# Cross attention of a decoder layer on one Trainium2 core: values and queries as three products of high and low parts, with the weights split on GpSimd

## Chip, core and metric

The kernel runs on one core of one Trainium2 chip. The metric is the time of one execution on the device, in microseconds (us). Three runs of the kernel before gave a median of 1062.45 us (1061.57 to 1063.77).

## The reference, cut to what matters

A decoder of two layers works on x (4 batches, 256 tokens, width 128) and a context (4 batches, 512 tokens, width 128). The first layer has a self attention, a cross attention with 16 heads of width 64, and a gated expert block with an attention of its own; the second has a self attention, a cross attention with one head and a mixture. All of it is float32. The change touches the first layer's cross attention alone. With m the normalised context and l the normalised latents (x after the self attention), both 128 wide, it computes

```
kv = concat([m, l], axis=1)                 # (4, 768, 128)
k, v = split(kv @ Wkv)                      # 16 heads of 64 each
q = (l @ Wq)                                # 16 heads of 64
out = softmax(q k^T / sqrt(64)) v           # per batch and head, 256 x 768 scores
y = concat(out) @ Wout
```

## The kernel before

The program is written per engine, with an own instruction list for TensorE, ScalarE, VectorE, GpSimd and the DMA queue of SyncE, and with semaphores between them. Everything lives in SBUF once the packed weights are loaded.

The cross attention is worked off in units. A unit is one pair of heads side (u % 2) of one batch (u // 2): 8 units make one pair of heads, and 8 pairs (XP) make the whole, so there are 64 units. `body(it, prev, cur)` in each engine's list writes out the 8 units of a pair; the first pair stands by itself, the next seven are a hardware loop, and a last partial body drains the pipeline.

Keys and queries of one head are folded into one 128 x 128 matrix per head (`A_all`, made once). A unit's query tile is that matrix times the latents; scores are the query tile times the keys' activations. On TensorE a unit consists of:

- `scores(u, half)` (lines 611 to 618), twice: each is two score tiles of 384 columns, each tile the sum of three products of type float32r (high x high, high x low, low x high), so 12 matmuls of 384 moving columns in a unit;
- `queries(it, u)` (lines 597 to 601), once: one float32 product of 256 moving columns with the stationary `acur`. A float32 matmul is two records in the trace;
- `values(it, b, half)` (lines 603 to 609), once: three float32 products, each with a tile of 128 tokens of `kvT` as stationary and 128 columns of the value weights `wv` moving, six records in the trace;
- `transposed` (lines 620 to 637): 12 transposes of 128 x 128 of the probabilities, one record each;
- in every second unit `weighted` (lines 639 to 648), 12 float32 products in two column halves of the array (24 records), and `factors`, two transposes.

`kvT` (float32) is split once, before the units: ScalarE rounds it to `kv_high` (line 1033), VectorE subtracts to make `kv_low` (line 1414, `key_low`), for each of the four batches. The query tile is split in the same way in each unit: ScalarE copies PSUM to `xq_high` (line 1061, for the first unit line 1026), VectorE makes `xq_low` (line 1408). VectorE also takes the maxima of the scores (line 1419), copies the values out of bank 7 (line 1424) and a third of the transposed probabilities (line 1445); ScalarE does the exponentials (line 1075) and the other two thirds (line 1066).

GpSimd's `cross()` (lines 1755 to 1767) copies the two matrices of the next pair of heads from `A_all` into `acur` (line 1761). Before and after, GpSimd's list holds small jobs of the normalisations (lines 1711 and 1712) and the masked queries of the self attentions (line 1726).

Two waits in front of the first unit matter for the change: the first `queries` and `values` wait for `kvT` alone, and the scores of batch b wait for `kv_split`, which counts the batches of which `kv_low` is there.

Of the kernel before, what the change touches and what calls it, by code (L numbers as in the profile page):

```python
# [14 lines left out]
B = 4  # L15
# [73 lines left out]
def decoder(nc, x_d, ctx_d, mask_d, packs_d, w1_d, w2_d, out_d):  # L89
# [4 lines left out]
    with ctx:  # L94
# [42 lines left out]
        ARENA = 17920  # L137
        arena = sb("arena", [P, ARENA])

# [35 lines left out]
        xprob = area(2, 2 * KEYS)  # L175

        xq_high = sb("xq_high", [P, 2, T], f32r)
        xq_low = sb("xq_low", [P, 2, T], f32r)
        acur = sb("acur", [P, 2, P])
# [149 lines left out]
        sx = family("x", "zT_psum", "zT_act", "zT_dve", "acur_ready", "q_psum", "q_high", "q_ready", "kv_high",  # L329
# [99 lines left out]
        def _(pe):  # L429
# [158 lines left out]
            def cross():  # L588
# [5 lines left out]
                wv, wo = col("v", "wv"), col("v", "wout")  # L594
                W = KEYS // 2

                def queries(it, u):

                    pe.wait_ge(sx["acur_ready"], it * 2 + u % 2 + 1)
                    mm(bank[6][:, T:2 * T], acur[:, u % 2, :], kvT[:, u // 2, S2:KEYS], start=True, stop=True)\  # L600
                        .then_inc(sx["q_psum"], 1)

                def values(it, b, half):

                    for k in range(3):
                        kt = 3 * half + k
                        last = mm(bank[7][:, k * P:(k + 1) * P], kvT[:, b, kt * P:(kt + 1) * P],  # L607
                                  wv[:, bass.ds(it * P, P)], start=True, stop=True)
                    last.then_inc(sx["v_psum"], 1)
# [46 lines left out]

                queries(0, 0)
                for half in range(2):
                    if half:

                        pe.wait_ge(sx["v_ready"], 1)
                    values(0, 0, half)

                def body(it, prev, cur):
                    for u in range(8):
# [3 lines left out]
                        if cur:  # L669
                            pe.wait_ge(sx["q_ready"], n + 1)  # L670
                            if prev or u:

                                pe.wait_ge(sx["exp_done"], n * 2 - 1)
                            if not prev and not odd:

                                pe.wait_ge(sx["kv_split"], b + 1)
                            scores(u, 0)
                            if odd:
                                queries(it + (u + 1) // 8, (u + 1) % 8)

                            pe.wait_ge(sx["v_ready"], n + 2)
                            values(it + (b + 1) // 4, (b + 1) % 4, odd)
# [235 lines left out]
        def _(act):  # L918
# [82 lines left out]
            def cross():  # L1001
# [23 lines left out]
                act.wait_ge(sx["q_psum"], 1)  # L1025
                activation(xq_high[:, 0, :], bank[6][:, T:2 * T], ACT.Copy).then_inc(sx["q_high"], 1)
                act.wait_ge(prep_act, 13)
                act.wait_ge(sx["zT_act"], 1)
                for b in range(B):
                    if b == 2:  # L1030

                        act.wait_ge(sx["zT_dve"], 1)
                    activation(kv_high[:, b, :], kvT[:, b, :], ACT.Copy).then_inc(sx["kv_high"], 1)
# [156 lines left out]
        def _(dve):  # L1190
# [211 lines left out]
            def cross_units():  # L1402
# [58 lines left out]
                v.memset(xrb[:, 0:1], 0.0).then_inc(sx["y_done"], 1)  # L1461
                query_low(1, 0)
                values(1, 0, 0)
                values(2, 0, 1)
                for b in range(B):
# [232 lines left out]
        def _(pool):  # L1698
            done = [0]

            def link(instruction):
                instruction.then_inc(pool_chain, 1)
                done[0] += 1
                pool.wait_ge(pool_chain, done[0])
# [50 lines left out]
            def cross():  # L1755
                def pair(it, prev):
                    for u in range(2):
# [3 lines left out]
                        pool.tensor_copy(acur[:, u, :], A_flat[:, bass.ds(it * 2 * P + u * P, P)])\  # L1761
# [3 lines left out]
                pair(0, False)  # L1765
                with pool.Fori(1, XP + 1) as it:
                    pair(it, True)

            pool.memset(half[:, :], -0.5).then_inc(pool_chain, 1)
            done[0] += 1  # L1770
            pool.wait_ge(pool_chain, 1)
# [99 lines left out]
```

## Time and profile before

| | |
|---|---|
| median of three runs | 1062.45 us |
| the profiled execution, its own time | 1061.55 us |
| its span in the trace | 1059.4 us |
| outside the span | 2.15 us |
| the cross attention's units (from the first scores to the last projection) | about 152 to 567 us of the span |
| a two-unit period in the loop | 12.38 us |

The span is what the profiler sees between the first and the last instruction. Times in the rows are microseconds from the start of the span. For TensorE the trace has two lines of events: PE for the matmuls and PEld for the loads of the stationary operand, which overlap. The duration of a matmul includes the depth of the pipeline, so the durations of neighbours overlap; what a matmul costs in a dense stretch is the distance from its start to the start of the next one. Below, that is called its pitch.

### The profile page before, as it was taken

How to read it: one execution, taken by the hardware profiler on the slowest of the kernel's cores; microseconds unless marked ns; L12 is line 12 of the kernel's file. 1: busy time of each engine (PE TensorE's matmuls, PEld its weight loads, DVE VectorE, ACT ScalarE, POOL GpSimd, SP SyncE). 2: the span in 40 equal slices, each digit the busy share in tenths (PEclk: the TensorE clock that was granted, in tenths of full speed). 3: DMA queues.
4: the chain of work that ended last, by engine and by line, in shares of the span. 5: the costliest groups of instructions: out<-in, count | busy, mean ns of one | idle time of the engine just before them, and what ended most of it. 6: DMA issues, size and time to landing. Idle time of an engine off the chain costs nothing.

```text
span 1059.4 us, 22196 instructions
## 1 busy us (share of the span) xinstructions
PE 979.9 (92%) x7108; PEld 800.9 (76%) x7108; DVE 685.9 (65%) x1715; ACT 573.2 (54%) x1511; POOL 176.3 (17%) x291
## 2 busy tenths in 40 slices
PE   5899979999999999999997999979999888888888
PEld 3677768888888888888884877768999665555665
DVE  5878666556666555666635788853222699999673
ACT  3676556555555555555531677745444376666440
POOL 3434120000000000000002333200000234443100
PEclk9999989999999999999998999999999899999995
DMA  6000000000000000000000000010110000000000
GB/s 254 1 1 0 1 1 1 1 1 1 0 0 0 0 0 0 0 0 0 0 1 0 2 0 0 0 50 21 40 40 30 1 1 0 0 0 0 21 1 20
DMA packets 6402, 12.95 MB, mean 12 GB/s; under 512 B 480, under 2 KB 2528, under 8 KB 5984
## 3 DMA queue, kind: packets, MB, share of 16 engines
q1 hardware_dynamic: 6368, 12.51, 3.5%
q8 instruction: 20, 0.33, 0.1%
q14 instruction: 14, 0.11, 0.0%
HBM read 11.98 MB, written 0.52 MB: 12 GB/s over the span
## 4 chain that ended last, share of the span: by engine, by line
PE 77%; DVE 13%; issue 5%; ACT 2%; DVEq 1%; DMA 1%; POOL 1%; SPq 0%; ACTq 0%
PE psum L504 9%; PE psum L635 8%; PE psum L647 8%; PE psum L769 6%; PE psum L615 5%; PE psum L523 4%; PE psum L617 4%; PE psum L616 4%; PE psum L607 4%; DVE arena L1296 4%; PE psum L600 3%; PE psum L541 3%; DVE arena L1274 2%; PE psum L753 2%; PE psum L754 2%
## 5 line engine op out<-in xcount | busy, mean ns | idle before, releaser
L1419 DVE TENSOR_REDUCE xnegmax<-psum 128x1 f32<-128x768 f32 x128 | 122.4, 956 | 138.5 <-PE psum L617 138.2
L1075 ACT ACTIVATE arena<-psum,xnegmax 128x768 f32<-128x768 f32 x128 | 115.5, 903 | 138.5 <-DVE xnegmax L1419 97.4
L504 PE MATMUL psum<-arena 128*128 (+2 forms) x768 | 187.0, 359 | 1.6 <-ACT arena L970 0.3
L1726 POOL TENSOR_TENSOR arena<-arena,pack_a 128x256 f32 (+1 forms) x192 | 122.6, 647 | 145.6 <-PE psum L508 70.6
L970 ACT ACTIVATE arena<-psum,arena 128x256 f32<-128x256 f32 (+1 forms) x256 | 112.3, 446 | 57.1 <-PE psum L523 26.4
L523 PE MATMUL psum<-pack_a,arena 128*128 128x128 f32 x704 | 110.6, 277 | 29.9 <-ACT arena L977 23.9
L504 PEld LDWEIGHTS psum<-arena 128*128 128x128 f32 x768 | 122.3, 192 | 11.0 <-issue 4.4
L523 PEld LDWEIGHTS psum<-pack_a,arena 128*128 128x128 f32 x704 | 79.3, 141 | 57.9 <-issue 24.2
L635 PE MATMUL psum<-pack_a,arena 128*128 128x128 f32 x768 | 106.8, 275 | 0.2 <-ACT arena L1066 0.2
L615 PE MATMUL psum<-kv_high,xq_high 128*128 128x384 f32 x256 | 101.1, 395 | 1.7 <-DVE kv_low L1414 1.6
L1066 ACT ACTIVATE arena<-psum 128x512 f32<-128x512 f32 x128 | 75.9, 593 | 42.4 <-PE psum L635 42.4
L635 PEld LDWEIGHTS psum<-pack_a,arena 128*128 128x128 f32 x768 | 87.3, 141 | 13.9 <-issue 12.3
L647 PE MATMUL psum<-arena,xv 128*64 128x256 f32 x768 | 89.9, 383 | 0.0
L617 PE MATMUL psum<-kv_high,xq_low 128*128 128x384 f32 x256 | 86.6, 338 | 0.0
L616 PE MATMUL psum<-kv_low,xq_high 128*128 128x384 f32 x256 | 86.5, 338 | 0.0
L1116 ACT ACTIVATE arena<-psum,pack_f 128x512 f32<-128x512 f32 x72 | 49.4, 688 | 60.0 <-PE psum L755 60.0
L769 PEld LDWEIGHTS psum<-arena 128*128 128x128 f32 x576 | 74.7, 191 | 6.1 <-DVE x L1535 0.3
L1303 DVE COPY arena<-psum 128x384 f32<-128x384 f32 (+1 forms) x96 | 59.0, 616 | 26.5 <-PE psum L523 26.5
L647 PEld LDWEIGHTS psum<-arena,xv 128*64 128x64 f32 x768 | 52.3, 137 | 31.0 <-issue 6.0
L769 PE MATMUL psum<-arena 128*128 128x128 f32 x576 | 75.4, 275 | 0.0
L1296 DVE SCALAR_TENSOR_TENSOR arena<-arena,ones_ 128x256 f32<-128x256 f32 x128 | 73.1, 573 | 0.1
L1761 POOL COPY acur<-A_all 128x128 f32 (+1 forms) x18 | 5.7, 321 | 386.4 <-PE psum L600 386.4
(238 smaller groups left out, 1810.1 us busy)
## 6 DMA issues: line engine op xcount, KB each, us to landing
arena<-in_w SPq DMA_DIRECT2D x18, 256.0 KB, 2.8
pack_v<-in_pack_v SPq DMA_DIRECT2D x1, 1088.0 KB, 9.6
pack_l<-in_pack_l SPq DMA_DIRECT2D x1, 1079.5 KB, 12.5
pack_q<-in_pack_q SPq DMA_DIRECT2D x1, 1024.0 KB, 7.4
pack_a<-in_pack_a SPq DMA_DIRECT2D x1, 649.0 KB, 6.2
pack_f<-in_pack_f SPq DMA_DIRECT2D x1, 625.0 KB, 10.6
pack_b<-in_pack_b SPq DMA_DIRECT2D x1, 578.0 KB, 9.3
x<-in_x SPq DMA_DIRECT2D x2, 256.0 KB, 3.2
```

The costliest lines, as they stand in the source:

```text
L504: last = mm(bank[j][:, u * T:u * T + keys], qm[:, j, u * P:(u + 1) * P], kT[:, bass.ds(b * T, keys)], start=True, stop=not a.causal)
L523: last = transpose(bank[4 + j % 2][:, i * P:(i + 1) * P], prob[:, j, u, k * P:(k + 1) * P], ident)
L615: mm(out, xq_high[:, u % 2, tile], kv_high[:, u // 2, keys], start=True, stop=False)
L616: mm(out, xq_high[:, u % 2, tile], kv_low[:, u // 2, keys], start=False, stop=False)
L617: last = mm(out, xq_low[:, u % 2, tile], kv_high[:, u // 2, keys], start=False, stop=True)
L635: last = transpose(bank[4 + (3 * u + c) % 2][:, (2 * i + h) * P:(2 * i + h + 1) * P], xprob[:, u % 2, h * KEYS + kt * P:h * KEYS + (kt + 1 ...
L647: mm(bank[6][XD * a:XD * (a + 1), 0:T], xv[:, b, kt * P + XD * a:kt * P + XD * (a + 1)], xpT[:, b % 2, a, kt * T:(kt + 1) * T], start=(kt ...
L769: last = mm(bank[2 * s + half][:, t * P:(t + 1) * P], hid[:, FT * half + f, t * P:(t + 1) * P], w2b[:, s, f * D:(f + 1) * D], start=(f == ...
L1075: activation(xprob[:, u % 2, half * KEYS:(half + 1) * KEYS].rearrange("p (c w) -> p c w", c=2), src, ACT.Exp, bias=xnegmax[:, u % 2, half: ...
L1296: v.scalar_tensor_tensor(prob[:, j, u, :], eraw[:, j, u, :], low[:, j, u:u + 1], ones[:, :], ALU.max, ALU.min, accum_out=sums[:, it, u * H ...
L1419: v.tensor_reduce(xnegmax[:, u % 2, half:half + 1], banks_pair(half), AX.XY, ALU.max, negate=True)\
L1726: pool.tensor_tensor(qm[:, j, :], qT[:, bass.ds(b * T, T)], headmask[:, bass.ds(g * HG + j, 1)].broadcast_to([P, T]), ALU.mult)\
```

## The change

`queries` becomes three float32r products (high x high, high x low, low x high) of 256 columns, and `values` becomes nine of 128 columns. They read `kv_high` and `kv_low` in place of `kvT`. The stationary of `queries` is now the split matrix `acur_high`/`acur_low`; the moving operand of `values` is the split weight `wcur`, of which there is one copy. Both splits are made on GpSimd: for each of the three 128 x 128 matrices of a pair, an exact copy (into `weff`, which is free by then), a rounding copy and a subtraction.

New waits: the first `queries` waits for `kv_split` 1 (before: for nothing but `kvT`), the values of the next batch in the first pair for `kv_split` b + 2, the values of the next pair (at u = 6) for `wcur_ready`; GpSimd waits for the last values of a pair (`v_psum`) before it overwrites `wcur`. On ScalarE the first query tile's copy moves behind `kv_high` of batch 0, and on VectorE `key_low(0)` moves ahead of the first query tile and the first two value copies.

```diff
@@ tiles
+        CROSS = 17408
+        with nc.sbuf_tensor("before_acur_low", [P, CROSS], f32), nc.sbuf_tensor("acur_low", [P, 2, P], f32r) as acur_low, \
+                nc.sbuf_tensor("wcur", [P, 2, P], f32r) as wcur:
+            pass
         arena = sb("arena", [P, ARENA])
...
-        acur = sb("acur", [P, 2, P])
+        acur_high = sb("acur_high", [P, 2, P], f32r)
@@ pe, cross()
                 def queries(it, u):
 
                     pe.wait_ge(sx["acur_ready"], it * 2 + u % 2 + 1)
-                    mm(bank[6][:, T:2 * T], acur[:, u % 2, :], kvT[:, u // 2, S2:KEYS], start=True, stop=True)\
+                    out, keys = bank[6][:, T:2 * T], slice(S2, KEYS)
+                    mm(out, acur_high[:, u % 2, :], kv_high[:, u // 2, keys], start=True, stop=False)
+                    mm(out, acur_high[:, u % 2, :], kv_low[:, u // 2, keys], start=False, stop=False)
+                    mm(out, acur_low[:, u % 2, :], kv_high[:, u // 2, keys], start=False, stop=True)\
                         .then_inc(sx["q_psum"], 1)
 
                 def values(it, b, half):
 
                     for k in range(3):
                         kt = 3 * half + k
-                        last = mm(bank[7][:, k * P:(k + 1) * P], kvT[:, b, kt * P:(kt + 1) * P],
-                                  wv[:, bass.ds(it * P, P)], start=True, stop=True)
+                        out, keys = bank[7][:, k * P:(k + 1) * P], slice(kt * P, (kt + 1) * P)
+                        mm(out, kv_high[:, b, keys], wcur[:, 0, :], start=True, stop=False)
+                        mm(out, kv_high[:, b, keys], wcur[:, 1, :], start=False, stop=False)
+                        last = mm(out, kv_low[:, b, keys], wcur[:, 0, :], start=False, stop=True)
                     last.then_inc(sx["v_psum"], 1)
...
+                pe.wait_ge(sx["kv_split"], 1)
                 queries(0, 0)
+                pe.wait_ge(sx["wcur_ready"], 1)
...
-                            if not prev and not odd:
-
-                                pe.wait_ge(sx["kv_split"], b + 1)
                             scores(u, 0)
+                            if not prev and not odd and b + 1 < B:
+
+                                pe.wait_ge(sx["kv_split"], b + 2)
                             if odd:
                                 queries(it + (u + 1) // 8, (u + 1) % 8)
 
                             pe.wait_ge(sx["v_ready"], n + 2)
+                            if u == 6:
+
+                                pe.wait_ge(sx["wcur_ready"], it + 2)
                             values(it + (b + 1) // 4, (b + 1) % 4, odd)
@@ act, cross()
-                act.wait_ge(sx["q_psum"], 1)
-                activation(xq_high[:, 0, :], bank[6][:, T:2 * T], ACT.Copy).then_inc(sx["q_high"], 1)
                 act.wait_ge(prep_act, 13)
                 act.wait_ge(sx["zT_act"], 1)
                 for b in range(B):
+                    if b == 1:
+                        act.wait_ge(sx["q_psum"], 1)
+                        activation(xq_high[:, 0, :], bank[6][:, T:2 * T], ACT.Copy).then_inc(sx["q_high"], 1)
@@ dve, cross_units()
                 v.memset(xrb[:, 0:1], 0.0).then_inc(sx["y_done"], 1)
+                key_low(0)
                 query_low(1, 0)
                 values(1, 0, 0)
                 values(2, 0, 1)
-                for b in range(B):
+                for b in range(1, B):
                     key_low(b)
@@ pool, cross()
+                wv, exact = col("v", "wv"), weff[:, :].rearrange("p (i c) -> p i c", i=3)
+
+                def weights(it, prev):
+
+                    if prev:
+
+                        pool.wait_ge(sx["v_psum"], it * 8)
+                    chain.did(pool.tensor_copy(exact[:, 2, :], wv[:, bass.ds(it * P, P)]))
+                    link(pool.tensor_copy(wcur[:, 0, :], wv[:, bass.ds(it * P, P)]))
+                    pool.tensor_tensor(wcur[:, 1, :], exact[:, 2, :], wcur[:, 0, :].bitcast(f32), ALU.subtract)\
+                        .then_inc(sx["wcur_ready"], 1)
+
                 def pair(it, prev):
                     for u in range(2):
                         if prev:
 
                             pool.wait_ge(sx["q_psum"], it * 8 - 1 + u)
-                        pool.tensor_copy(acur[:, u, :], A_flat[:, bass.ds(it * 2 * P + u * P, P)])\
+                        now = A_flat[:, bass.ds(it * 2 * P + u * P, P)]
+                        chain.did(pool.tensor_copy(exact[:, u, :], now))
+                        link(pool.tensor_copy(acur_high[:, u, :], now))
+                        pool.tensor_tensor(acur_low[:, u, :], exact[:, u, :], acur_high[:, u, :].bitcast(f32), ALU.subtract)\
                             .then_inc(sx["acur_ready"], 1)
 
                 pool.wait_ge(prep_act, 5)
                 pair(0, False)
+                pool.wait_ge(loaded["v"], 16)
+                weights(0, False)
                 with pool.Fori(1, XP + 1) as it:
+                    chain.enter(it, 1, 6)
+                    weights(it, True)
                     pair(it, True)
+                    chain.leave(XP)
```

## Rows read from the trace of the kernel before

**Rows 1.** The page, busy time by engine: us (share of the span) x instructions.
```profile
PE 979.9 (92%) x7108; PEld 800.9 (76%) x7108; DVE 685.9 (65%) x1715; ACT 573.2 (54%) x1511; POOL 176.3 (17%) x291
```

**Rows 2.** Windows, 160 to 540 us: length, PE, PEld, DVE, ACT, POOL, PEclk, DMA.
```profile
160.00:540.00 380.00, 379.81 (x2760) 328.57 (x2759) 229.82 (x402) 208.28 (x463) 4.74 (x16) 1.00 0.00 0
```

**Rows 3.** Waits in 160 to 540 us: who waited for whom, us, times, longest.
```profile
DVE xnegmax L1419 <- PE psum L617: 137.4, 93, 3.6
...
PEld psum L635 <- issue: 11.5, 30, 0.4
...
PEld psum L647 <- ACT arena L1066: 1.7, 7, 0.2
```

**Rows 4.** Timeline of PE in the loop: start, duration, line, operands, records.
```profile
455.74 2.81 PE L647 MATMUL psum<-arena,xv 128*64 128x256 f32 x24
...
465.01 0.59 PE L600 MATMUL psum<-kvT,acur 128*128 128x256 f32 x2
465.44 0.83 PE L607 MATMUL psum<-pack_v,kvT 128*128 x6
466.11 1.04 PE L635 MATMUL psum<-pack_a,arena 128*128 128x128 f32 x8
...
467.16 0.34 PE L616 MATMUL psum<-kv_low,xq_high 128*128 128x384 f32 x1
...
467.86 0.34 PE L617 MATMUL psum<-kv_high,xq_low 128*128 128x384 f32 x1
468.12 1.08 PE L647 MATMUL psum<-arena,xv 128*64 128x256 f32 x8
```

**Rows 5.** Timeline, the expert gate's matmuls of 10 moving columns and their successor.
```profile
711.68 1.86 PEld L733 LDWEIGHTS psum<-pack_f,zT 128*128 128x128 f32 x16 [1.25 <-ACT zT L932]
...
713.46 0.19 PEld L753 LDWEIGHTS psum<-z_high,w_high 128*128 128x128 f32 x1
```

**Rows 6.** Groups of weight loads by line and shape: busy us, mean ns of one.
```profile
L647 PEld LDWEIGHTS psum<-arena,xv 128*64 128x64 f32 x768 | 52.3, 137 | 31.0 <-issue 6.0 <-ACT arena L1066 1.7
L616 PEld LDWEIGHTS psum<-kv_low,xq_high 128*128 128x128 f32 x256 | 48.6, 190 | 0.8
L615 PEld LDWEIGHTS psum<-kv_high,xq_high 128*128 128x128 f32 x256 | 48.5, 189 | 5.7 <-issue 1.8 <-DVE xq_low L1408 0.4
...
L541 PEld LDWEIGHTS psum<-arena 128*32 128x32 f32 x768 | 20.3, 109 | 21.2 <-issue 6.6 <-DVE arena L1303 5.8 <-ACT arena L977 0.2
...
L508 PEld LDWEIGHTS psum<-causalb,identb 128*128 128x128 bf16 x256 | 25.4, 99 | 3.3
```

**Rows 7.** Timeline of PE in the experts: float32r products of 512 moving columns.
```profile
727.41 0.39 PE L754 MATMUL psum<-z_low,w_high 128*128 128x512 f32 x1
...
727.65 0.39 PE L755 MATMUL psum<-z_high,w_low 128*128 128x512 f32 x1
...
727.88 1.05 PE L769 MATMUL psum<-arena 128*128 128x128 f32 x8
```

**Rows 8.** Timeline of all engines around the first query and value products.
```profile
145.21 0.99 POOL L1761 COPY acur<-A_all 128x128 f32<-128x128 f32 x2
...
147.76 0.67 PE L600 MATMUL psum<-kvT,acur 128*128 128x256 f32 x2 [0.95 <-DVE kvT L1399]
...
148.75 3.03 ACT L1033 ACTIVATE kv_high<-kvT 128x768 fp32r<-128x768 f32 x4
...
150.80 0.56 DVE L1424 COPY xv<-psum 128x384 f32<-128x384 f32 x1 [1.03 <-PE psum L607]
151.27 3.55 DVE L1414 TENSOR_TENSOR kv_low<-kvT,kv_high 128x768 fp32r<-128x768 f32 x4
...
154.75 0.95 DVE L1419 TENSOR_REDUCE xnegmax<-psum 128x1 f32<-128x768 f32 x1
```

**Rows 9.** GpSimd's copies of 128 x 128: duration ns min/median/max.
```profile
L1761 POOL COPY acur<-A_all x18: 292/296/759, 145.2 to 537.0; 128x128 f32 x16, 128x128 f32<-128x128 f32 x2
```

**Rows 10.** GpSimd's products of 128 x 256: duration ns min/median/max.
```profile
L1726 POOL TENSOR_TENSOR arena<-arena,pack_a x192: 607/614/1076, 16.0 to 970.9; 128x256 f32 x168, 128x256 f32<-128x256 f32 x24
```

More of the change, by code:

```diff
@@ L175, in decoder @@
         xprob = area(2, 2 * KEYS)
+        assert area.at <= CROSS
         xq_high = sb("xq_high", [P, 2, T], f32r)
         xq_low = sb("xq_low", [P, 2, T], f32r)
-        acur = sb("acur", [P, 2, P])
+        acur_high = sb("acur_high", [P, 2, P], f32r)
         xnegmax = sb("xnegmax", [P, 2, 2])
@@ L327, in family @@
             return {n: sem(f"{tag}_{n}") for n in names}
-        sx = family("x", "zT_psum", "zT_act", "zT_dve", "acur_ready", "q_psum", "q_high", "q_ready", "kv_high",
+        sx = family("x", "zT_psum", "zT_act", "zT_dve", "acur_ready", "wcur_ready", "q_psum", "q_high", "q_ready", "kv_high",
                     "kv_split", "v_psum", "v_ready",
@@ L593, in cross @@
                 pe.wait_ge(loaded["v"], 16)
-                wv, wo = col("v", "wv"), col("v", "wout")
+                wo = col("v", "wout")
                 W = KEYS // 2
@@ L1698, in _ @@
         def _(pool):
-            done = [0]
+            chain = Chain(pool_chain)
             def link(instruction):
-                instruction.then_inc(pool_chain, 1)
-                done[0] += 1
-                pool.wait_ge(pool_chain, done[0])
+                chain.did(instruction)
+                chain.wait(pool)
             def rstd_jobs(keys):
@@ L1765, in cross @@
                 pair(0, False)
+                pool.wait_ge(loaded["v"], 16)
+                weights(0, False)
                 with pool.Fori(1, XP + 1) as it:
+                    chain.enter(it, 1, 6)
+                    weights(it, True)
                     pair(it, True)
-            pool.memset(half[:, :], -0.5).then_inc(pool_chain, 1)
-            done[0] += 1
-            pool.wait_ge(pool_chain, 1)
+                    chain.leave(XP)
+            link(pool.memset(half[:, :], -0.5))
             rstd_jobs(FIRST_JOBS)
```

## Prediction

> **What bounds the kernel now.** I read the page's busy shares first: TensorE 92%, the other engines 65% and less [rows 1]. A share over the whole span does not say what bounds one stage, so next the stretch of the cross attention's loop: in 380 us PE is busy 379.8, VectorE 230, ScalarE 208, GpSimd 5, and the granted clock is 1.00, the upper level of 2.4 GHz [rows 2]. The waits of the same stretch say it more clearly: VectorE waits 137 us for TensorE's scores, while TensorE's loads of weights wait for another engine only 1.7 us in total; its other idle time, 11.5 us in front of the transposes, is its own issue [rows 3]. So TensorE bounds the loop, nothing is queued in front of it, and what the change adds or takes in a unit shows in the end time. What counts is therefore the pitch of its instructions, start to start, from the timeline [rows 4].
>
> **The pitches of now.** A values call is six records: 466.11 - 465.44 = 0.67 us, 0.112 each. A queries call takes 465.44 - 465.01 = 0.43 us. A float32r product of 384 columns, with its own load, has a pitch of (467.86 - 467.16)/4 = 0.175 us [rows 4], one of 512 columns 0.235 (727.88 - 727.41 over two) [rows 7]: both are 0.457 ns a column, so at these widths the columns set the pitch.
>
> **What the change does to queries.** Three products of 256 columns: by 0.457 ns a column an estimate of 0.117 us each, 0.35 in all, against 0.43: -0.08 us a unit.
>
> **What it does to values.** Nine products of 128 columns in place of six records, and this is the disputed term. The columns alone would give 9 x 0.058 = 0.53 us. But each product loads its own 128 x 128 stationary, and the trace shows what such a load costs where the moving side is almost nothing: the expert gate's 16 records with 10 moving columns take 713.46 - 711.68 = 1.78 us, 0.111 each [rows 5]. Those are float32 loads. Is a float32r load cheaper? Loads of 128, 64 and 32 columns last 190, 137 and 109 ns [rows 6]: 0.84 ns a column on some 82 ns of fixed latency, so 128 columns occupy the path for 0.108 us, which is the pitch again; and the 190 ns is that of float32r (the scores' lines 615 and 616). The one fast load, 99 ns, is bf16 [rows 6]. Neither does a shared stationary help: the scores' first two products have the same stationary, and the trace holds 256 loads for each of the two lines [rows 6]. So I take 9 x 0.111 = 1.00 us against 0.67: +0.33 us a unit. The ends are 0.058 a product (the column rate, 0.53 a call) and 0.222 (a float32r product as slow as the two float32 records of the same shape [rows 4], 2.0 a call); 0.111 is nearest to both a load and a record of this shape.
>
> Two rules speak otherwise. The Trainium skill, "TensorE: Matmul & The Clock Gate", section "Weight-path perf modes", says that the fast weight load is used for 128 weights when the type is not FP32; if float32r counted as such, the loads would vanish behind the columns and the sum would be that of rival A. The float32r loads' 190 ns beside the 99 ns of bf16 speak against it. The same page, "Back-to-back issue gap", gives about 81 ns for a pair of load and matmul of 128 columns in a real kernel; by it a values call would take 0.73 us and the loop would end within 2 us of today. That is rival B.
>
> **The loop's sum.** (+0.33 - 0.08) x 64 units = +16.0 us. The number of changes between float32 and float32r neighbours stays the same, so I take nothing for them. VectorE and ScalarE get no more work in a unit, and have idle time behind TensorE [rows 3]; the values' copy comes 0.33 us later after TensorE's start, before scores that are as much later.
>
> **GpSimd** gets nine instructions a pair in place of two. Copies of this size take 0.296 us [rows 9]; a product of twice the size 0.614 [rows 10], so a subtraction about 0.31, at most 0.61. The value weights have one buffer: their split can only start when the values of unit 5 are done and must end before those of unit 6. It takes 2 x 0.30 + 0.31 = 0.9 us, 1.2 with the upper end. Between the two calls lie at least 468.12 - 466.11 = 2.0 us and then 24 records of `weighted`, 2.75 us: 4.7 us [rows 4]. The query matrices' split is queued behind it on GpSimd, is due only at unit 7, and costs another 0.9 each. Cover: TensorE's transposes, scores and `weighted`; if a step were late, TensorE would stand still once a pair for the difference. I take nothing.
>
> **The start.** Today `queries` start at 147.76, when `kvT` is there [rows 8]. Now they wait for `kv_high` of batch 0 (3.03/4 = 0.76 us on ScalarE) and `kv_low` (3.55/4 = 0.89 on VectorE): +1.65 us. Two values calls follow one behind the other, through one bank: 2 x 0.33 more. Of the `key_low` calls ahead of the first maximum (154.75 [rows 8]) one is already done: -0.89. Together +1.4 us. GpSimd's first nine instructions start at 145.21 [rows 8] and take some 3 to 4 us, done at about the time at which the first values want them. Ends: 0 (the first units are full of gaps that may take it up) and +4 (two values calls at half the clock, another 1 us each, and GpSimd late by half a us).
>
> **Sum:** +16.0 + 1.4 = +17.4 us on the profiled execution's own time of 1061.55 (span 1059.4 and 2.15 around it), which lies 0.9 below the median. Against the median, 1062.45 + 17.4 = 1079.9 us.
>
> **Rivals.**
> A, faster: the float32r product of 128 columns goes at its column rate, 0.058 us, the load being hidden. Its place is the values call on TensorE; -0.14 - 0.08 = -0.22 a unit, -14.3 + 1.4: 1049.5 us. It decides below a pitch of (0.67 + 0.08)/9 = 0.083 us. For: 384 and 512 columns do run at column rate. Against: rows 5 and 6.
> B, no change: load and product overlap partly, at about the pitch of 0.083 at which the gain of the queries pays for the values: +0 to 2 us, about 1063. Only the cited page speaks for it; the trace has no pair with a full load of this type under 0.11.
> C, much slower: a float32r product of few columns falls back to two slow passes, 0.222 us. +1.33 - 0.08 = +1.25 a unit, +80: 1144 us. Against: nothing at 384 columns hints at it. For: no row has fewer.
> D, GpSimd late: the rounding copies are far slower than plain ones. At 3 us an instruction the split takes 9 us against 4.7 to 6, TensorE stands 3 to 4 us for each of eight pairs: about +28 on top, 1108 us. Against: rows 9 and 10.
>
> **How the numbers follow.** The load-bound case 0.80, A 0.06, B 0.03, C 0.07, D 0.04. The load-bound case's own range: below, the start costs nothing, two or three units are hidden in its gaps and the load counts 0.108 us: some +12 to +14, 1075; above, load and product disturb each other by the 9% that the 384-column pitch (0.175) has over 384 columns at 2.4 GHz (0.160): 0.121 a product, +0.42 - 0.07 = +0.35 a unit, 22.4 + 4 = +26, 1089. I give 1071 to 1090, which holds nearly all of this case and a mild form of D, 0.81 in all. Such a kernel's measurement tells about 0.2%, 2 us, from no change: faster 0.06, same 0.03, slower 0.91.
>
> **What the profile of the changed kernel would show.** Right: nine records of `values` in about 1.0 us and three of `queries` in 0.35; a two-unit period of 12.38 + 0.5 = 12.9 us; PE still without waits in the loop and its clock at 1.00; loads of `values` of 190 ns each; VectorE's wait for the scores longer by some 15 us. The first scores about 1 us later. Wrong: a values call of 0.55 us and a period near 12.0 (A), of 0.75 and 12.4 (B), of 2 us and 15 (C), or an idle TensorE in front of unit 6's values, ended by GpSimd (D). A fall of the granted clock in the loop would make every term too small.

## The result, and the profile after

The changed kernel takes 1076.3 us (median of four runs, 1074.7 to 1077.7) against 1062.8 for the kernel before in the same job: a ratio of 1.0127, 95% interval 1.0109 to 1.0146, so 11.6 to 15.5 us slower. The forecast was 1079.9 us, in a range of 1071 to 1090; 91% stood on slower. The profiled execution has a span of 1072.9 us, 13.5 more than before.

The page, busy time by engine, answers to [rows 1]:

```profile
PE 992.2 (92%) x7371; PEld 821.5 (77%) x7371; DVE 690.7 (64%) x1715; ACT 572.2 (53%) x1511; POOL 197.7 (18%) x354
```

TensorE is busy 12 us longer and has 263 more records; GpSimd is busy 21 us longer, VectorE 5, ScalarE as it was. The same stretch of the loop as [rows 2], with the columns of there, and its waits, which answer to [rows 3]:

```profile
160.00:540.00 380.00, 378.98 (x2931) 337.75 (x2930) 229.47 (x393) 203.15 (x452) 20.32 (x63) 1.00 0.00 0
```

```profile
DVE xnegmax L1435 <- PE psum L627: 134.1, 90, 3.6
...
PEld psum L645 <- issue: 11.2, 29, 0.4
```

TensorE is full as before, at the same granted clock of 1.00. VectorE's wait for the scores, which I had expected to grow by some 15 us, did not: 134.1 us against 137.4. The timeline of PE in the loop, which answers to [rows 4] (L606 to L608 are the three query products, L616 to L618 the nine value products, L645 the transposes, L657 `weighted`):

```profile
451.29 0.28 PE L606 MATMUL psum<-kv_high,acur_high 128*128 128x256 f32 x1
...
451.64 0.23 PE L616 MATMUL psum<-wcur,kv_high 128*128 128x128 f32 x1
451.70 0.27 PE L617 MATMUL psum<-wcur,kv_high 128*128 128x128 f32 x1
451.81 0.28 PE L618 MATMUL psum<-wcur,kv_low 128*128 128x128 f32 x1
...
452.60 1.06 PE L645 MATMUL psum<-pack_a,arena 128*128 128x128 f32 x8
...
454.64 2.81 PE L657 MATMUL psum<-arena,xv 128*64 128x256 f32 x24
...
467.28 2.81 PE L657 MATMUL psum<-arena,xv 128*64 128x256 f32 x24
```

A queries call takes 451.64 - 451.29 = 0.35 us, a values call 452.60 - 451.64 = 0.96, with a pitch of 0.11 between its products; only the first takes 0.06. Its load began at 451.52, under the last query product. The two-unit period is 467.28 - 454.64 = 12.64 us, against 12.38. The groups of weight loads in 160 to 540 us answer to [rows 6]:

```profile
L626 PEld LDWEIGHTS psum<-kv_low,xq_high 128*128 128x128 f32 x244 | 46.2, 189 | 0.0
...
L616 PEld LDWEIGHTS psum<-wcur,kv_high 128*128 128x128 f32 x180 | 34.3, 191 | 0.0
```

The value products' loads last 191 ns, the scores' 189: the same load.

Where the 13.5 us lie, by rows of the chain of waits (first and last mark of each stage: the first self attention's projection, the first block of `weighted`, the cross attention's projection):

```profile
123.27 3.57 PE psum L575 x32
...
171.07 2.74 PE psum L647 x24
...
548.06 7.15 PE psum L716 x64
```

```profile
125.61 3.57 PE psum L580 x32
...
176.38 2.74 PE psum L657 x24
...
561.44 7.15 PE psum L731 x64
```

The first fence is before, the second after. Up to the first mark +2.34 us, in a stage that the change does not touch. From there to the first `weighted` 47.80 and 50.77: +2.97. From there to the projection 376.99 and 385.06: +8.07. Behind it 511.34 and 511.46: +0.12. The first difference is scatter: over the traces of this study that mark lies between 123.1 and 125.6 us, whatever the kernel. The whole time scatters too (the kernel before ran from 1058.2 to 1065.1 us in 23 runs of one job), and the granted clock in stretches outside the loop differs between traces. So the experiments below are read by stage first, and by the ratio second.

### The profile page after: what moved, and what is told of

Read it like the earlier page. It is cut to its first block, busy times and chain, and to the rows that moved or that the text cites. A ratio compares the mean times of both kernels' runs of the same rounds, so it can differ in the third digit from the quotient of the medians.

```text
span 1072.9 us, 22822 instructions
## 1 busy us (share of the span) xinstructions
PE 992.2 (92%) x7371; PEld 821.5 (77%) x7371; DVE 690.7 (64%) x1715; ACT 572.2 (53%) x1511; POOL 197.7 (18%) x354
## 4 chain that ended last, share of the span: by engine, by line
PE 78%; DVE 12%; issue 4%; ACT 2%; DVEq 1%; DMA 1%; POOL 1%; SPq 0%; ACTq 0%
PE psum L509 10%; PE psum L645 8%; PE psum L657 8%; PE psum L784 6%; PE psum L528 5%; PE psum L625 4%; PE psum L626 4%; PE psum L627 4%; DVE arena L1312 4%; PE psum L546 3%; PE psum L618 2%; PE psum L617 2%; PE psum L616 2%; PE psum L768 2%; PE psum L769 2%
## 5 line engine op out<-in xcount | busy, mean ns | idle before, releaser
L528 PEld LDWEIGHTS psum<-pack_a,arena 128*128 128x128 f32 x704 | 79.4, 142 | 58.1 <-issue 24.5
L645 PE MATMUL psum<-pack_a,arena 128*128 128x128 f32 x768 | 108.2, 277 | 0.2 <-ACT arena L1082 0.2
L625 PE MATMUL psum<-kv_high,xq_high 128*128 128x384 f32 x256 | 95.5, 373 | 1.0 <-DVE xq_low L1424 1.0
L645 PEld LDWEIGHTS psum<-pack_a,arena 128*128 128x128 f32 x768 | 84.2, 140 | 13.8 <-issue 12.3
L657 PE MATMUL psum<-arena,xv 128*64 128x256 f32 x768 | 90.0, 383 | 0.0
L657 PEld LDWEIGHTS psum<-arena,xv 128*64 128x64 f32 x768 | 52.3, 137 | 31.1 <-issue 7.9
L1779 POOL COPY weff<-pack_v 128x128 f32 (+1 forms) x9 | 2.6, 292 | 320.8 <-PE psum L618 320.8
```

The source lines that it names most:

```text
L528: last = transpose(bank[4 + j % 2][:, i * P:(i + 1) * P], prob[:, j, u, k * P:(k + 1) * P], ident)
L625: mm(out, xq_high[:, u % 2, tile], kv_high[:, u // 2, keys], start=True, stop=False)
L645: last = transpose(bank[4 + (3 * u + c) % 2][:, (2 * i + h) * P:(2 * i + h + 1) * P], xprob[:, u % 2, h * KEYS + kt * P:h * KEYS + (kt + 1 ...
L657: mm(bank[6][XD * a:XD * (a + 1), 0:T], xv[:, b, kt * P + XD * a:kt * P + XD * (a + 1)], xpT[:, b % 2, a, kt * T:(kt + 1) * T], start=(kt ...
```

## The experiments

All numbers of the loop are means over the 23 to 25 periods between 200 and 500 us of each trace, taken from the start times in the timeline. "Even block" is the stretch of the even unit from the eight transposes through queries, second scores and four transposes to the next scores.

| kernel | time, us | ratio to before (95%) | period | values call | even block | start |
|---|---|---|---|---|---|---|
| before | 1062.8 | | 12.39 | 0.667 | 2.97 | 47.8 |
| after | 1076.3 | 1.0127 (1.0109-1.0146) | 12.65 | 0.955 | 2.68 | 50.8 |
| cols64 | 1076.6 | 1.0134 (1.0110-1.0157) | 12.65 | 0.922 | 2.72 | 51.0 |
| merged | 1063.0 | 0.9995 (0.9979-1.0011) | 12.32 | 0.641 | 2.98 | 50.1 |
| q_only | 1062.2 | 0.9997 (0.9983-1.0011) | 12.32 | 0.665 | 2.95 | 48.6 |
| v_only | 1078.0 | 1.0144 (1.0120-1.0167) | 12.79 | | 2.75 | 53.4 |
| start_only | 1064.6 | 1.0026 (1.0011-1.0040) | 12.40 | 0.667 | 2.97 | 48.9 |
| pool_only | 1064.8 | 1.0022 (1.0010-1.0033) | 12.40 | 0.668 | 2.96 | 48.3 |
| filler | 1067.6 | 1.0041 (1.0027-1.0055) | 12.52 | 0.778 | 2.86 | 48.1 |
| cut_before | 1059.9 | 0.9972 (0.9961-0.9984) | 12.29 | 0.667 | 2.87 | 48.3 |
| cut2_before | 1057.1 | 0.9948 (0.9933-0.9963) | 12.16 | 0.667 | 2.72 | 47.7 |
| cut2_after | 1075.2 | 1.0124 (1.0106-1.0143) | 12.65 | 0.955 | 2.68 | 50.9 |
| best | 1061.3 | 0.9978 (0.9964-0.9993) | 12.33 | 0.666 | 2.96 | 47.8 |
| best2 | 1062.8 | 0.9999 (0.9989-1.0010) | 12.41 | 0.667 | 3.03 | 47.5 |

The first two rows are of one job; in the jobs of the others the kernel before had medians of 1062.7 to 1063.2, and each ratio is to its own job. "Start" is the time from the first self attention's projection to the first `weighted`, by the chain of waits of each trace. In `v_only` the boundary between queries and values in the odd unit isn't comparable, so its values call is left out.

### Load or columns

`cols64`:

```diff
-                        mm(out, kv_high[:, b, keys], wcur[:, 0, :], start=True, stop=False)
+                        mm(out, kv_high[:, b, keys], wcur[:, 0, 0:XD], start=True, stop=False)
...
```

(and so for the other two products).

> The changed kernel with 64 instead of 128 moving columns in each of the nine value products (the other half of each pair's values is left out); everything else, the loads of 128 x 128 stationary tiles too, is the same. Theory (a product of 128 columns costs its load, 0.106 us a product in the changed kernel's loop): the values call stays at 0.95 us, the two-unit period at 12.65 us, the time at 1076 us within 2. Rival (narrow float32r products are slow by the column, 0.83 ns each at this width): the call halves to 0.5 us, the period falls by 0.9 us, the time to about 1048 us.

Measured: the same period and time as the changed kernel, 12.65 and 1076.6 us. The timeline of PE in the loop of `cols64`:

```profile
451.44 0.19 PE L616 MATMUL psum<-wcur,kv_high 128*128 128x64 f32 x1
451.47 0.28 PE L617 MATMUL psum<-wcur,kv_high 128*128 128x64 f32 x1
451.58 0.28 PE L618 MATMUL psum<-wcur,kv_low 128*128 128x64 f32 x1
...
452.36 1.09 PE L645 MATMUL psum<-pack_a,arena 128*128 128x128 f32 x8
```

The pitch of products of 64 columns is 0.11 us, that of 128 columns. (The call counts as 0.92 us in the table, 0.03 less, and the transposes behind it take 0.03 more.) The rival falls: half the columns buy nothing, the product costs its load. The Trainium skill, "TensorE: Matmul & The Clock Gate", section "LDWEIGHTS (loading the stationary operand)", gives the number of stationary columns over 1.2 GHz, 107 ns for 128; the trace agrees within 5%, with 0.955 us over nine products of the changed kernel, 0.106 each, or 0.112 for the eight behind the short first one. The 81 ns for a pair of load and product of 128 columns that the Trainium skill gives on the same page, section "Back-to-back issue gap", is not what these rows show for float32r.

`merged` joins the two products that share their stationary tile:

```diff
-                        out, keys = bank[7][:, k * P:(k + 1) * P], slice(kt * P, (kt + 1) * P)
-                        mm(out, kv_high[:, b, keys], wcur[:, 0, :], start=True, stop=False)
-                        mm(out, kv_high[:, b, keys], wcur[:, 1, :], start=False, stop=False)
-                        last = mm(out, kv_low[:, b, keys], wcur[:, 0, :], start=False, stop=True)
+                        out, keys = bank[7][:, k * P:(k + 2) * P], slice(kt * P, (kt + 1) * P)
+                        mm(out, kv_high[:, b, keys], wcur[:, :, :].rearrange("p i c -> p (i c)"), start=True, stop=False)
+                        last = mm(out[:, 0:P], kv_low[:, b, keys], wcur[:, 0, :], start=False, stop=True)
```

> The changed kernel with the first two value products, which share their stationary tile, as one of 256 moving columns (high and low weights side by side; the low half lands beside its place and is not added, so the output lacks it). Same 9 x 128 columns streamed, six loads in place of nine. Theory (each load costs 0.106 to 0.111 us where it is not covered by columns): a call takes 3 x (0.117 + 0.06 to 0.11) = 0.55 to 0.68 us, the period falls from 12.65 to about 12.0 to 12.1, the time to 1057 to 1060 us. Rival (the columns set the time): 1076 us.

Measured: 0.641 us a call, six loads at 0.107, with as many columns as before. The period falls only to 12.32 where 12.65 - 2 x 0.314 = 12.02 was due. The missing 0.30 us is in the even block, which grew back from 2.68 to 2.98 us though nothing of it was edited. So the loop holds a wait that a long values call hides.

### Each part alone

`q_only`: the value products, `wcur_ready` and the weights' split as before, the rest as changed. `v_only`: the reverse.

```diff
# q_only, against the changed kernel
-                        mm(out, kv_high[:, b, keys], wcur[:, 0, :], start=True, stop=False)
...
+                        last = mm(bank[7][:, k * P:(k + 1) * P], kvT[:, b, kt * P:(kt + 1) * P],
+                                  wv[:, bass.ds(it * P, P)], start=True, stop=True)
# v_only, against the changed kernel
-                    mm(out, acur_high[:, u % 2, :], kv_high[:, u // 2, keys], start=True, stop=False)
...
+                    mm(bank[6][:, T:2 * T], acur[:, u % 2, :], kvT[:, u // 2, S2:KEYS], start=True, stop=True)\
```

> The changed kernel with the values as before (float32 from kvT and wv, six records a call); queries as three products, GpSimd splits the query matrices alone, start as changed. If only the products' own pitch counts (-0.08 us a unit, start +1.4): 1059 us. If, as the two traces together suggest, a float32 product between float32r or transposed neighbours in the even units costs more than its own time (the even unit's queries and what stands on both sides of them lost 0.20 us, the odd unit's 0.08), the period falls from 12.39 to 12.11 us and the time to 1055 us.

> The changed kernel with the queries as before (float32, acur from GpSimd, kvT); values as nine products. If the terms add up as in my sum (values +0.29 a unit, no gain of the queries): 1076 + 5 = 1081 us, period 12.8 us. If the change of type costs about 0.1 us each time that a float32r product follows a float32 one, as the even unit of before shows, the odd unit gains another such place (queries float32, then values float32r): period 12.98 us, 1084 us.

Both of my numbers for `q_only` fail, the second one clearly: 12.32 us a period in place of 12.11. The odd unit's queries gained 0.08 us as computed; the even block gained 0.02 in all, though its queries and the following scores are shorter by 0.08 together. For `v_only` the period of 12.79 is the additive one (12.8), and the whole time is 1078, below both numbers; the change of type as a cost of 0.1 us falls with it. Against the kernel before, though, the period grew by 0.40 where two longer value calls alone make 0.58, and again the even block is short (2.75). The 0.20 us that I had put down to the type had another cause.

### The hidden waits

The timeline of the kernel before in one even unit, all engines:

```profile
460.91 1.04 PE L635 MATMUL psum<-pack_a,arena 128*128 128x128 f32 x8
461.32 0.41 DVE L1428 TENSOR_TENSOR arena<-psum,xrb 128x256 f32 x1
...
461.78 0.30 PEld L600 LDWEIGHTS psum<-kvT,acur 128*128 128x128 f32 x2
...
462.41 0.59 ACT L1066 ACTIVATE arena<-psum 128x512 f32<-128x512 f32 x1
...
462.89 0.38 ACT L1061 ACTIVATE xq_high<-psum 128x256 fp32r<-128x256 f32 x1
...
463.30 0.42 DVE L1408 TENSOR_TENSOR xq_low<-psum,xq_high 128x256 fp32r<-128x256 f32 x1
463.37 0.60 PE L635 MATMUL psum<-pack_a,arena 128*128 128x128 f32 x4
...
463.85 0.19 PEld L615 LDWEIGHTS psum<-kv_high,xq_high 128*128 128x128 f32 x1
463.86 0.44 PE L615 MATMUL psum<-kv_high,xq_high 128*128 128x384 f32 x1
```

Two of TensorE's starts sit right behind another engine. The queries' load (461.78) follows the end of VectorE's scaling of the outputs (461.32 + 0.41 = 461.73), for whose `y_done` they wait. The next unit's scores (463.85) follow the end of `xq_low` (463.30 + 0.42 = 463.72) by 0.13, and `xq_low` stands at the end of a chain: scores, maximum, exponential, ScalarE's copy of transposed probabilities (462.41), its copy of the query tile (462.89). In the changed kernel:

```profile
460.22 0.41 DVE L1444 TENSOR_TENSOR arena<-psum,xrb 128x256 f32 x1
...
460.89 0.19 PEld L606 LDWEIGHTS psum<-kv_high,acur_high 128*128 128x128 f32 x1
...
462.22 0.42 DVE L1424 TENSOR_TENSOR xq_low<-psum,xq_high 128x256 fp32r<-128x256 f32 x1
...
462.41 0.60 PE L645 MATMUL psum<-pack_a,arena 128*128 128x128 f32 x4
...
462.77 0.19 PEld L625 LDWEIGHTS psum<-kv_high,xq_high 128*128 128x128 f32 x1
```

the scaling ends at 460.63 and the queries load at 460.89, when TensorE has come to them, and the four transposes before the next scores take 0.36 us in place of 0.49. Here too the scores' load comes 0.13 after the end of `xq_low` (462.64), but the transposes' loads have only just ended: the chain has no room left. So a start right behind another engine's end does not yet show lost time; the runs below have to.

Hardly any of this is named in the list of waits [rows 3]. A matmul's record lasts 0.27 to 0.5 us, so a gap of 0.1 us in its issue is covered by the records of its predecessors; on the line of the loads the gaps are 0.07 and 0.12 us, and the list has nothing as short. One sign of it was there, in the lists over 160 to 540 us, first the kernel before, then `q_only` (L623 is the scores):

```profile
PEld psum L600 <- issue: 1.8, 7, 0.3
```

```profile
PEld psum L623 <- issue: 4.1, 21, 0.2
```

I had taken "issue" for TensorE's own time. The seven gaps of 0.26 us in front of the queries, one in each pair of heads, are gone in `cut2_before`, where VectorE's scaling comes earlier, so they were a wait; and the gaps in front of the scores in `q_only` end 0.13 us after an `xq_low`.

`filler` is the kernel before with one unused transpose in each values call:

```diff
                 def values(it, b, half):
 
+                    transpose(bank[7][:, 3 * P:4 * P], ident, ident)
                     for k in range(3):
```

> The kernel before with one unused transpose of 128 columns (0.111 us, into the free quarter of bank 7) ahead of the products of each values call. If TensorE's order hides nothing: +0.111 x 66 = 7.3 us, 1070.1 us, period 12.61 us. If in part of the even units the scores wait for the query tile that ScalarE and VectorE make (0.49 instead of 0.36 us for the four transposes ahead of them, 0.085 us a period in the mean), and a longer values call gives that chain time, as in the changed kernel, this wait goes: period 12.53 us, 1067.5 us.

Measured 12.52 us and 1067.6: of 0.222 us that were added to a period, 0.13 arrive, and the even block shrinks by 0.11. Where it shrinks is not where I had put it: the four transposes stay at 0.44 us (from 0.455), and queries with what follows fall from 1.586 to 1.515, so it was mostly the wait for `y_done` that shrank.

`cut_before` and `cut2_before` take the waits away without adding to TensorE's work:

```diff
# cut_before, ScalarE
-                    activation(xpT[:, (mu // 2) % 2, mu % 2, 2 * c * T:2 * (c + 1) * T], bank[4 + (3 * mu + c) % 2][:, :],
+                    w = 2 * T if c or mu % 2 == 0 or isinstance(m, int) else P
+                    activation(xpT[:, (mu // 2) % 2, mu % 2, 2 * c * T:2 * c * T + w], bank[4 + (3 * mu + c) % 2][:, 0:w],
                                ACT.Copy).then_inc(sx["pT_act"], 1)
# cut2_before and cut2_after, in addition, VectorE
+                        if not odd and (prev or u >= 4):
+                            results(it * 4 + b - 2, it - (u < 4), (b - 2) % 4)
                         if cur:
                             maxima(n, u, 0)
                             if odd:
                                 query_low(n + 2, (u + 1) % 2)
-                        if not odd and (prev or u >= 4):
-                            results(it * 4 + b - 2, it - (u < 4), (b - 2) % 4)
```

> The kernel before, where ScalarE's first copy of transposed probabilities in every even unit of the loop takes 128 of its 512 columns (the rest is left out, about 0.3 us less in front of the query tile's copy). Theory of hidden waits (part of the even unit's second scores wait for the query tile that ScalarE and VectorE make, 0.10 us a period in the mean): the four transposes ahead of these scores fall from 0.455 to 0.35 us, the period from 12.39 to 12.29, the time by 3 us to 1060. Rival (TensorE does not wait there, the 0.49 us is its own change of type): nothing moves.

> As the run before, and VectorE's scaling of the finished outputs stands ahead of the maxima of the even units, so that y_done, for which the even unit's queries wait, comes early. Theory: both hidden waits go, 0.216 us a period, without any change of TensorE's work: period 12.17 us, time 1056.5 us. If only the first wait is one: 12.29 us as in the run before.

> The same two edits in the changed kernel. Theory: the longer value calls have taken up both waits already, so nothing is left to gain: period 12.65 us, 1076 us, within 0.03 and 1.5. If the edits help by themselves: 12.43 us, 1069 us.

All three came out as the theory has them: 12.29, 12.16 and 12.65 us a period, 1059.9, 1057.1 and 1075.2 us. With less work on ScalarE alone the four transposes fall from 0.455 to 0.356 us; with the scaling earlier too, the queries' part falls from 1.586 to 1.486 and the transposes ahead of it from 0.925 to 0.874. The same edits do nothing in the changed kernel. This also tests my sum without the waits: from `cut2_before` to `cut2_after`, the change adds 0.49 us to a period (12.16 to 12.65), 0.25 a unit as forecast, and 18 us to the time (1057.1 to 1075.2), where it adds 0.26 and 13.5 with the waits in place. The timeline of PE in `cut2_before`, one even unit (L600 queries, L635 transposes, L615 scores):

```profile
444.65 1.04 PE L635 MATMUL psum<-pack_a,arena 128*128 128x128 f32 x8
...
445.52 0.60 PE L600 MATMUL psum<-kvT,acur 128*128 128x256 f32 x2
...
447.01 0.60 PE L635 MATMUL psum<-pack_a,arena 128*128 128x128 f32 x4
...
447.40 0.43 PE L615 MATMUL psum<-kv_high,xq_high 128*128 128x384 f32 x1
```

From the eight transposes to the next scores it is 447.40 - 444.65 = 2.75 us here; in the kernel before it is 463.86 - 460.91 = 2.95.

### The start, and GpSimd

`start_only` is the kernel before with the three edits of order (PE's wait for `kv_split` 1, ScalarE's and VectorE's lists). `pool_only` is the kernel before with GpSimd's part of the change; its queries read GpSimd's exact copies.

```diff
# start_only, against the kernel before
+                pe.wait_ge(sx["kv_split"], 1)
                 queries(0, 0)
...
+                key_low(0)
                 query_low(1, 0)
# pool_only, against the changed kernel
+                    mm(bank[6][:, T:2 * T], weff[:, (u % 2) * P:(u % 2 + 1) * P], kvT[:, u // 2, S2:KEYS], start=True, stop=True)\
```

> The kernel before with the order of the start changed alone: queries(0, 0) waits for kv_split 1, ScalarE makes kv_high of batch 0 before the first query tile, VectorE key_low(0) first. All products float32. By the traces the queries start 1.3 us later and one key_low of 0.89 is already done when the maxima come: +0.4 to +1.4 us, 1063.5 to 1064.5; the period stays 12.39 us. If instead the 3 us that the changed kernel lost between kvT and its third unit come from this order (TensorE idle and then at the lower clock), most of them appear here: 1065 to 1066 us. If they come from the nine products of each of the first value calls at the lower clock, they do not.

> TensorE, ScalarE and VectorE as in the kernel before (float32 queries from the exact copies that GpSimd makes, values from kvT and wv, start as before), GpSimd with all nine splitting instructions of a pair and its waits. If GpSimd's work is covered, as I forecast: no change, 1062.8 us within 1, period 12.39 us. If it takes memory bandwidth from VectorE or comes late at the start (the wcur split ended 0.06 us before the first value product in the changed kernel): +0.3 to +1 us.

By the traces the start takes 48.9 us with the new order and 48.3 with GpSimd's part, against 47.8. One trace each measures it only roughly: `cut_before`, which is edited in the loop alone and starts like the kernel before, has 48.3 too: its second values call took 1.45 us in place of 0.94. TensorE's granted clock in 155 to 160 us is 0.61 there and 0.89 in the kernel before:

```profile
155.00:160.00 5.00, 5.00 (x20) 4.74 (x20) 4.16 (x6) 1.33 (x3) 0.00 (x0) 0.61 0.00 0
```

So some 0.5 us of a start can be the clock's, without any edit, and the order (clock 0.68 in its trace) costs between 0.5 and 1.1. GpSimd's 0.5 is a wait that its trace names: the first value product starts 0.95 us behind the queries (148.23), 0.51 in the kernel before, and waits for the split of the weights:

```profile
149.18 0.94 PE L612 MATMUL psum<-pack_v,kvT 128*128 128x128 f32 x6 [0.28 <-POOL wcur L1773]
```

In the loop GpSimd costs nothing (12.40). The whole times, 1064.6 and 1064.8 us, are at or above the top of what I had expected, and the ratios say 2.8 us (1.2 to 4.3) and 2.3 (1.1 to 3.5): larger than the stage shows. Part of each is time outside the cross attention, or scatter that the intervals do not hold; what of it belongs to the edits stays open. The rest of the changed kernel's +3.0 is in its own timeline (columns as in [rows 8]):

```profile
149.21 0.84 ACT L1049 ACTIVATE kv_high<-kvT 128x768 fp32r<-128x768 f32 x1
...
150.08 1.05 DVE L1430 TENSOR_TENSOR kv_low<-kvT,kv_high 128x768 fp32r<-128x768 f32 x1
150.26 1.02 POOL L1780 CAST wcur<-pack_v 128x128 fp32r<-128x128 f32 x1
151.36 0.46 POOL L1781 TENSOR_TENSOR wcur<-weff,wcur 128x128 fp32r<-128x128 f32 x1
...
151.41 0.36 PE L606 MATMUL psum<-kv_high,acur_high 128*128 128x256 f32 x1 [2.32 <-DVE kv_low L1430]
...
151.88 0.33 PE L616 MATMUL psum<-wcur,kv_high 128*128 128x128 f32 x1
...
154.25 0.48 PE L616 MATMUL psum<-wcur,kv_high 128*128 128x128 f32 x1 [0.65 <-DVE xv L1440]
...
156.23 0.63 PE L625 MATMUL psum<-kv_high,xq_high 128*128 128x384 f32 x1
```

`kv_low` of batch 0 takes 1.05 us beside GpSimd (0.96 in `start_only`) and ends at 151.13. The queries start at 151.41, 1.3 us later than in [rows 8] once the 2.34 us of shift ahead of this stage are taken off. The second values call begins at 154.25 and the scores behind it at 156.23, 1.98 us for nine products: a pitch of 0.21 behind the first. TensorE's granted clock is lower in the stretch 155 to 160 us than it was, here after and before:

```profile
155.00:160.00 5.00, 5.00 (x25) 5.00 (x25) 3.53 (x5) 0.00 (x0) 0.00 (x0) 0.58 0.00 0
```

```profile
155.00:160.00 5.00, 4.90 (x29) 4.41 (x28) 3.76 (x6) 2.68 (x7) 0.00 (x0) 0.89 0.02 3
```

0.58 here, at the lower level of 1.2 GHz for most of it, 0.89 before. At the lower level the nine products of a call cost about 2 us. It is again the load that they pay for: in `cols64`, products of 64 columns have the same pitch of 0.21 there (153.95 to 155.66 over eight). Why the clock was low for longer is not shown. TensorE had stood for 2.3 us in front of the queries, but in `cut_before` it had stood for only 0.95 there, as before the change, and was at 0.61 all the same. `v_only`, in whose trace the clock was 0.64 in 147 to 155 us and 0.50 in 155 to 160, has the longest start of all, 53.4.

### Toward a better version

`best` is `q_only` with the first two value calls ahead of the first queries, and VectorE's list in that order:

```diff
# against q_only
+                for half in range(2):
+                    if half:
+
+                        pe.wait_ge(sx["v_ready"], 1)
+                    values(0, 0, half)
                 pe.wait_ge(sx["kv_split"], 1)
                 queries(0, 0)
-                for half in range(2):
...
+                values(1, 0, 0)
                 key_low(0)
-                query_low(1, 0)
-                values(1, 0, 0)
                 values(2, 0, 1)
+                query_low(1, 0)
```

> Queries as three products, values float32 as before, and the start put in another order: the first two value calls, which need kvT alone, run ahead of queries(0, 0), so that the wait for kv_low of batch 0 is covered. If the even unit loses 0.20 us by the new queries: period 12.11 us, no cost at the start, 1053.5 us. If only the products' own pitch counts: 12.23 us, 1057.5 us.

> The three-product queries with float32 values and the reordered start, and in addition VectorE's scaling ahead of the maxima in the even units (complete and correct by its data flow). If the chain scores - maximum - exponential - copy - query tile bounds the even unit, the wait moves from the queries to the second scores and little is gained: period 12.30 us within 0.03, 1061 us. If the wait for y_done was the longer one by itself: period 12.2 us, 1057.5 us.

`best` has the lowest median of the complete kernels, 1061.3 us, a ratio of 0.9978 (0.9964 to 0.9993): 0.7 to 3.8 us faster than before, and 2 us by its stages (31 periods of 0.06). Its start costs nothing (47.8); the loop gives the 12.33 us of `q_only`, for the same reason. Both of my numbers for it, 1053.5 and 1057.5, were too low. `best2` moves VectorE's scaling ahead as `cut2_before` does, without cutting ScalarE's copy, and gives it back: the wait moves to the second scores, as its expectation says, and grows: 12.41 us a period where I had expected 12.30. The timeline of `best2` in an even unit:

```profile
447.57 0.42 DVE L1438 TENSOR_TENSOR arena<-psum,xrb 128x256 f32 x1 [3.42 <-ACT xrb L1064]
...
450.76 0.42 DVE L1418 TENSOR_TENSOR xq_low<-psum,xq_high 128x256 fp32r<-128x256 f32 x1 [0.32 <-ACT xq_high L1071]
...
451.32 0.44 PE L623 MATMUL psum<-kv_high,xq_high 128*128 128x384 f32 x1 [0.15 <-DVE xq_low L1418]
```

The scaling ends at 447.99, the maximum stands behind it and starts the chain some 0.1 us later than in `best`, and the scores (L623) now show a wait for `xq_low`. The four transposes ahead of them take 0.75 us against 0.52. Untried is a product with 256 moving columns made of the weights of two pairs, six loads a call without the loss of the low part; it needs twice the room for the values.

## Why the prediction was right

**The bound and the sign.** Right. TensorE bounds the loop, but for the waits below; a float32r product of 128 columns costs its load, and nine of them cost more than six float32 records. `cols64` shows the load as the cause; rivals A (0.058 us), B (0.083) and C (0.222) fall to the measured pitch of 0.106 to 0.111.

**Values, +0.33 us a unit.** Measured +0.29: the second product of a call starts 0.06 us after the first, whose load the columns ahead of the call cover, and I had charged nine full loads.

**Queries, -0.08 a unit.** Right where TensorE alone decides: the odd unit's went from 0.43 to 0.35 us.

**"Nothing is queued in front of it, and what the change adds or takes in a unit shows in the end time."** This step failed. Of +0.25 us forecast for a unit, +0.13 arrived (12.39 to 12.65 over two units). The even block lost 0.29 us where the queries' own gain is 0.08 of it at most. The other 0.2 were two waits in the even unit, for `y_done` and for the query tile; the longer value calls took them up. I had read the list of waits as complete and its "issue" as TensorE's own time, and so put these waits at nothing. In the loop that is 0.1 us x 64 = some 6.5 us; the value term's 0.04 makes another 2.7, and small lengthenings of transposes and scores gave about 1.5 back. That they are waits is shown by `cut2_before` (0.23 us less a period with the same work on TensorE) and `cut2_after` (nothing); between these two the change costs the 0.25 us a unit of my sum.

**GpSimd, nothing in the loop.** Right: 12.40 us with all its work; rival D falls. At the start the rounding copy of the weights took 1.02 us and the split ended at 151.82, 0.06 before the first value product; in `pool_only`, whose queries start earlier, the split was late and cost some 0.5.

**The start, +1.4 us.** Measured +3.0, inside my bounds of 0 to 4. The order costs 0.5 to 1.1 of it and the clock by itself up to 0.5. The term that was too small is the value calls, 0.33 us more each by my sum: at the lower clock the second one took 1.98 us. I had that as the upper end.

The sum of +17.4 was 3.9 too high against the medians' 13.5. By stage it was further off: +11.0 in the cross attention, the loop 16.0 against 8.1, the start 1.4 against 3.0. In the profiled pair 2.3 us of shift ahead of this stage, which the change does not explain, make up for some of the loop's 7.9. So the nearness of the total is in part luck; the sign and the bound are not.

## What to carry to other kernels

In a run of products with a stationary tile of 128 columns each, a product costs the tile's load, here 0.106 to 0.112 us, whether 64 or 128 columns move; splitting a narrow float32 product into three pays only where the moving side is wide enough to cover three loads, as it was with 256 columns and was not with 128. An engine whose records touch each other is not thereby free of waits, and a gap that the profile puts down to "issue" can be one: compare the starts of its instructions with the ends of what they wait for, in each kind of unit, before assuming that time added or removed there arrives at the end. And a gain on such an engine can vanish into a chain over the other engines that was nearly as long.

## What the runs showed that I had not expected

Loads of neighbours share their cover: in `merged` a product of 128 columns behind one of 256 takes 0.06 us, the next of 256 then 0.17 (means of its loop); a call's three pairs take 0.214 us each, two loads. At the lower clock a load-bound product took twice as long, 0.21 us, with 128 columns as with 64. The same program scattered by 7 us over 23 runs. In the trace of `q_only` the stretch from 559 to 698 us had a granted clock of 0.98 and the one from 990 us to the end 0.89, where the kernel before shows 0.95 and 0.81.
